# Second cross-attention in scaled half-precision parts, and its sum products behind a chunk's fourth score

## What is computed

```
x = x + tanh(g_xattn[0]) * L0_xattn(ln(x), ctx, mask)    # one head of 512, masked
x = x + tanh(g_ffn[0])   * L0_ffn(ln(x), w_up, w_down)   # Hadamard, 8 bit, ternary weights
x = x + tanh(g_xattn[1]) * L1_xattn(ln(x), ctx)          # 16 heads of channels
x = x + tanh(g_ffn[1])   * L1_ffn(ln(x), w1, w2, w3)     # silu(a) * b, NF4 weights
```

```
q = qkv.reshape(bs * 16, ch, length)
k = v = y.reshape(bs * 16, ch, -1)
scale = 1.0 / math.sqrt(math.sqrt(ch))
weight = softmax(einsum('bct,bcs->bts', q * scale, k * scale))
a = einsum('bts,bcs->bct', weight, v)
```

## Time and profile before

| | us |
|---|---|
| three runs | 1840.54, 1842.40, 1844.35 |
| median | 1842.4 |
| the profiled execution, its own time | 1841.3 |
| its span, first to last instruction | 1839.5 |
| PE busy in the span | 1658.9 (90%) |
| DVE, POOL, ACT busy | 1147.0, 843.0, 760.9 |
| mean granted clock of PE | 0.959 |

### The profile page before, as it was taken

How to read it: one execution, slowest core, us unless ns; L and a number is a source line. 1 busy time by engine, 2 the same in 40 slices (tenths; PEclk the granted TensorE clock), 3 DMA queues, 4 the chain that set the end, 5 groups by cost and what they waited for, 6 DMA issues and landing times. The chain is left out here.

```text
span 1839.5 us, 22129 instructions
## 1 busy us (share of the span) xinstructions
PE 1658.9 (90%) x7540; PEld 800.2 (44%) x7568; DVE 1147.0 (62%) x1529; ACT 760.9 (41%) x1241; POOL 843.0 (46%) x340
## 2 busy tenths in 40 slices
PE   5999999898777876899999999899999997799898
PEld 2454444444433333444444444444444432344443
DVE  3669989884455557676766676667676630444543
ACT  1321211211543431566666666566666665111110
POOL 0022234544221125577778888677777877000000
PEclk9999999899899995999999999999999999799999
DMA  8232223322111115444333334444433310400000
GB/s 320 80 120 77 83 93 96 103 100 79 39 30 35 34 41 137 113 114 112 77 96 89 98 97 113 114 113 113 113 88 90 77 46 1 95 23 0 23 23 23
DMA packets 134316, 152.57 MB, mean 83 GB/s; under 512 B 59694, under 2 KB 101826, under 8 KB 134214
## 3 DMA queue, kind: packets, MB, share of 16 engines
q1 hardware_dynamic: 129222, 140.76, 29.3%
q10 hardware_dynamic: 4992, 10.49, 1.7%
HBM read 73.42 MB, written 10.76 MB: 46 GB/s over the span
## 5 line engine op out<-in xcount | busy, mean ns | idle before, releaser
L1352 DVE TENSOR_REDUCE c_piece_max<-c_unit 128x1 f32<-128x804 f32 x512 | 485.0, 984 | 241.0 <-PE c_unit L1490 238.4
L1448 ACT ACTIVATE c_prob<-c_scores 128x512 f32<-128x512 f32 (+1 forms) x832 | 473.3, 596 | 267.3 <-PE c_scores L1507 250.5
L1287 POOL TENSOR_TENSOR c_prob_sum<-c_prob_sum,c_prob 128x2048 f32<-128x2048 f32 x96 | 439.4, 4577 | 12.0 <-ACT c_prob L1448 6.0
L1507 PE MATMUL c_scores<-c_queries,c_keys 98*128 98x512 f32 (+1 forms) x832 | 354.8, 443 | 32.7 <-ACT c_prob L1448 17.4
L1490 PE MATMUL c_unit<-c_khigh,c_qdiag 128*128 128x402 f32 x1024 | 303.2, 381 | 20.1 <-DMA c_qdiag<-c_qhigh 10.1
L1490 PEld LDWEIGHTS c_unit<-c_khigh,c_qdiag 128*128 128x128 f32 x1024 | 186.6, 198 | 150.1 <-DVE c_piece_max L1352 90.1
L1507 PEld LDWEIGHTS c_scores<-c_queries,c_keys 98*128 98x128 f32 (+1 forms) x832 | 152.4, 186 | 202.0 <-ACT c_prob L1448 141.3
L1516 PE MATMUL c_out<-c_prob,c_VT 128*32 128x512 f32 (+1 forms) x1664 | 220.8, 610 | 0.0
L641 PE MATMUL a_S<-a_ctxT,a_xnT 128*128 128x401 f32 x512 | 190.7, 517 | 7.2 <-ACT a_prob L598 3.9
L671 PE MATMUL a_o<-a_ctx,a_probT 128*128 128x512 f32 (+1 forms) x416 | 181.2, 592 | 0.0
L1287 POOL TENSOR_TENSOR c_prob_sum<-c_prob 128x2048 f32<-128x2048 f32 x16 | 73.5, 4592 | 121.1 <-ACT c_prob L1448 121.1
(11 more groups left out here) (196 smaller groups left out, 1975.0 us busy)
## 6 DMA issues: line engine op xcount, KB each, us to landing
c_keys<-c_khigh SPq DMA_DIRECT2D x128, 200.2 KB, 3.0
c_k<-in_keys SPq DMA_DIRECT2D x16, 801.0 KB, 6.3
c_keys<-c_k SPq DMA_DIRECT2D x64, 200.2 KB, 3.0
a_ctx<-in_ctx SPq DMA_DIRECT2D x12, 1024.0 KB, 6.8
c_VT<-in_values SPq DMA_DIRECT2D x16, 768.0 KB
a_ctxT<-in_ctxT SPq DMA_DIRECT2D x12, 802.0 KB, 4.7
c_queries<-c_qhigh SPq DMA_DIRECT2D x128, 64.0 KB, 2.6
a_weights<-in_L_ffn_weight SPq DMA_DIRECT2D x3, 1408.0 KB, 14.7
```

The source lines that it names most:

```text
L1287: nc.gpsimd.tensor_tensor(psum4[:], a[:], prob[(j * MC + c) % RING][:], ALU.add).then_inc(sums_taken, 2 if i == 1 else 1)
L1352: nc.vector.tensor_reduce(piece_max[j % 2][:, k // 2, k % 2:k % 2 + 1], U[bank(unit)][:, :, 0:PIECE], axis=AX.XY, op=ALU.max).then_inc(uni ...
L1448: nc.scalar.activation(prob[(j * MC + c) % RING][0:w, h, :], STp[h % 2][0:w, :], ACT.Exp, scale=SCALE).then_inc(exp_done, 1)
L1507: nc.tensor.matmul(STp[h % 2][0:w, :], K[p][:, h, c * P:c * P + w].bitcast(F32R), Q[p][:, h, :].bitcast(F32R), start=True, stop=True).then ...
```

## The change

1. In cross_attention_1 the tiles khigh, krest, qhigh, qrest, the query diagonal (QZ), K, Q and nrow are float16 in place of 32-bit types. krest no longer lies in the keys' own buffer. There is one row for the maxima in place of two (ones become 2^9, the row is divided by it), and no splitting of the maxima on ACT and POOL; `c_nmax` goes to PE.
2. So that the keys fit float16, they are multiplied by a scale of the whole context, 2^13 over its largest absolute value. ACT does so as it makes khigh; the exp gets its scale from a [128, 1] tile in place of a constant.
3. The scale is made in cross_attention_0: `context_top(b)` on DVE, for each batch, a transfer to memory and back over the partitions, and `context_scales()`, four small DVE operations. `load_transposed(b)` on SP waits for `context_top(b - 1)`.
4. `rest_of_k` goes from POOL to DVE: one scalar_tensor_tensor, in a slot's unit stream behind pair 6 of the group g+2. It is made in slots 0 to 13, and for groups 0 and 1 before them.
5. The sum products of a chunk in SUMMED go from behind its value products (after the second score) to behind the fourth score. The last chunk's stay.

The core of the diff:

```diff
-        krest = [k[:].bitcast(F32R) for k in kt]
-        khigh = [sb(f"c_khigh{j}", [P, MK], F32R) for j in range(2)]
+        krest = [sb(f"c_krest{j}", [P, MK], F16) for j in range(2)]
+        khigh = [sb(f"c_khigh{j}", [P, MK], F16) for j in range(2)]
...
+            def context_top(b):
+                for n in range(4):
+                    dve.wait_ge(ctxT_loaded[n], 16 * (b + 1))
+                nc.vector.tensor_reduce(ctx_tops[:, b:b + 1], CT[:], axis=AX.XY, op=ALU.max, apply_absolute_value=True).then_inc(ctx_topped, 1)
+                if b == B - 1:
+                    dve.wait_ge(ctx_topped, B)
+                    nc.vector.tensor_reduce(ctx_tops[:, B:B + 1], ctx_tops[:, 0:B], axis=AX.X, op=ALU.max).then_inc(ctx_topped, 1)
...
                 if k > 1:
                     add_out(k - 2)
+                if k % ST == 2:
+                    context_top(k // ST)
...
             add_out(K - 2)
+            context_scales()
...
-            def rest_of_k(n, j):
-                pool.wait_ge(khigh_ready, n + 1)
-                nc.gpsimd.tensor_tensor(krest[j], kt[j][:], khigh[j][:], ALU.subtract).then_inc(rests_ready, 1)
...
+            def rest_of_k(n, j):
+                dve.wait_ge(khigh_ready, n + 1)
+                wait(dve, stacked, (n - 1) * STACKS)
+                nc.vector.scalar_tensor_tensor(krest[j][:], kt[j][:], key_scale, khigh[j][:], ALU.mult, ALU.subtract).then_inc(krest_ready, 1)
...
+                    if main and more and unit[2:] == (j + 2, 6):
+                        rest_of_k(g + 2, j % 2)
...
-                nc.scalar.copy(khigh[j][:], kt[j][:]).then_inc(khigh_ready, 1)
+                nc.scalar.activation(khigh[j][:], kt[j][:], ACT.Copy, scale=key_scale).then_inc(khigh_ready, 1)
...
-                    nc.scalar.activation(prob[(j * MC + c) % RING][0:w, h, :], STp[h % 2][0:w, :], ACT.Exp, scale=SCALE).then_inc(exp_done, 1)
+                    nc.scalar.activation(prob[(j * MC + c) % RING][0:w, h, :], STp[h % 2][0:w, :], ACT.Exp, scale=score_scale[0:w]).then_inc(exp_done, 1)
...
-                        if h == 1:
-                            for b in outs.get(c, [c - 1]):
-                                out_and_den(g, j, b)
+                        for b in outs.get(c, [c - 1]):
+                            if h == 1:
+                                out_alone(g, j, b)
+                            elif h == 3:
+                                den_alone(g, j, b)
```

More of the change, by code:

```diff
@@ L1259, in rest_of_q @@
                 wait(pool, stacked, n * STACKS)
[L1260 to L1269 removed]
+                nc.gpsimd.tensor_tensor(qrest[:], xn[:], qhigh[j][:], ALU.subtract).then_inc(qrest_ready, 1)
             def add_gain(g):
@@ L1291, in _ @@
             rest_of_q(0, 0)
-            rest_of_k(0, 0)
             steps.link(pool.memset(QZ[1][:], 0.0))
@@ L1295, in _ @@
             rest_of_q(1, 1)
-            rest_of_k(1, 1)
             steps.link(pool.memset(ones32[:], 1.0))
             for j in range(2):
-                steps.link(pool.memset(K[j][KM:KA, :, :], 1.0))
-            rest_of_maxima(0)
+                steps.link(pool.memset(K[j][KM:KA, :, :], ONES))
             normalize(2)
@@ L1320, in slot @@
                     rest_of_q(g + 2, j % 2)
-                    rest_of_k(g + 2, j % 2)
             every_slot(pool, slot)
@@ L1361, in keep_rows @@
                 dve.wait_ge(unit_full, FULL0 + rows_place(n) + 1)
-                nc.vector.tensor_copy(nrow[:], U[bank(unit)][0:2 * H, 0, :]).then_inc(unit_read, 1)
+                nc.vector.tensor_scalar(nrow[:], U[bank(unit)][0:H, 0, :], 1.0 / ONES, None, ALU.mult).then_inc(unit_read, 1)
                 dve.wait_ge(unit_read, UNITS0 + rows_place(n) + 1)
@@ L1374, in _ @@
             statistics(1)
+            rest_of_k(0, 0)
             def slot(g, j, main, nxt, more, later):
@@ L1395, in slot @@
                         moments_done(g + 3)
+                    if main and more and unit[2:] == (j + 2, 6):
+                        rest_of_k(g + 2, j % 2)
                 if not main:
+                    rest_of_k(1, 1)
                     statistics(2)
@@ L1424, in split_queries @@
                 nc.scalar.copy(qhigh[j][:], xn[:]).then_inc(qhigh_ready, 1)
-            def high_of_maxima(n):
-                act.wait_ge(nmax_ready, n + 1)
-                wait(act, unit_full, FULL0 + rows_place(n - 1) + 1 if not isinstance(n, int) or n > 0 else 0)
-                nc.scalar.copy(nparts[:].bitcast(F32R)[:, :, :, 0].rearrange("p t h -> p h t"), nmax[:]).then_inc(nhigh_ready, 1)
             def take_out(g):
@@ L1465, in slot @@
                         split_keys(g + 2, j % 2)
-                    if c == (8 if not isinstance(g, int) or g > 0 else 10) and nxt:
-                        high_of_maxima(g + 1)
                 if nxt:
@@ L1489, in pair @@
                     at = STARTS[2 * half + e]
-                    last = nc.tensor.matmul(U[bank(unit)][:, e, 0:PIECE], QZ[o][:, h, t * P:(t + 1) * P].bitcast(F32R), khigh[o][:, at:at + PIECE], start=True, stop=True)
+                    last = nc.tensor.matmul(U[bank(unit)][:, e, 0:PIECE], QZ[o][:, h, t * P:(t + 1) * P], khigh[o][:, at:at + PIECE], start=True, stop=True)
                 last.then_inc(unit_full, 1)
@@ L1494, in rows @@
                 n = unit[1]
-                pe.wait_ge(nparts_ready, n + 1)
+                pe.wait_ge(nmax_ready, n + 1)
                 pe.wait_ge(unit_read, rows_place(n) + 1)
                 for t in range(TB):
-                    last = nc.tensor.transpose(U[bank(unit)][0:2 * H, 0, t * P:(t + 1) * P], nparts[:, t, :, :].rearrange("p h a -> p (h a)"), ident[:])
+                    last = nc.tensor.transpose(U[bank(unit)][0:H, 0, t * P:(t + 1) * P], nmax[:, t, :], ident[:])
                 last.then_inc(unit_full, 1)
@@ L1506, in score @@
                 pe.wait_ge(exp_done, g * EXPS + H * c + h + 1)
-                nc.tensor.matmul(STp[h % 2][0:w, :], K[p][:, h, c * P:c * P + w].bitcast(F32R), Q[p][:, h, :].bitcast(F32R), start=True, stop=True).then_inc(scores_ready, 1)
+                nc.tensor.matmul(STp[h % 2][0:w, :], K[p][:, h, c * P:c * P + w], Q[p][:, h, :], start=True, stop=True).then_inc(scores_ready, 1)
             def out(g, j, c):
@@ L1533, in den_of_sum, with out_alone, den_alone @@
                 last.then_inc(den_done, 1)
-            def out_and_den(g, j, c):
+            def out_alone(g, j, c):
                 last = out(g, j, c)
+                if c not in SUMMED:
+                    last.then_inc(pv_done, 1)
+            def den_alone(g, j, c):
                 if c in SUMMED:
-                    last = den(g, j, c)
-                last.then_inc(pv_done, 1)
+                    den(g, j, c).then_inc(pv_done, 1)
             def slot(g, j, main, nxt, more, later):
```

76 lines of the change are left out of this document (46 added, 30 removed).

## The result

The changed kernel takes 1863.14 us (median of 4 runs, 1861.71 to 1868.29) against 1841.89 us for the kernel before in the same comparison: a ratio of 1.0119, interval 1.0097 to 1.0141. It is slower by 21 us; 35 were forecast, and the range held it. The profiled execution took 1863.7 us, its span is 1861.9, 22.4 more than before.

A forecast was written before the change was run, and what follows sets the result against it. PE's order and exposed waits were taken to set the pace, POOL next. 1841.3 + 13.5 (cross_attention_0) - 5 (start) - 4 (slot 0) - 5 (slots 14, 15) + 37 (slots 1 to 13) = 1877.8, recorded as 1877; range 1808 to 1889.

The forecast's parts named there:

- The hold: Slots 1 to 13: DVE's rest-of-keys instruction waits for POOL's add-up, PE stands still 3.9 us; +3.65 us a slot.
- the rival that DVE slips through (B): cross_attention_1 slots: DVE isn't held by POOL's add-up, its 1.8 us hides in PE's two banks; 1812.2 us, chance 0.28.
- The clock: Slots 1 to 13: PE's stop brings its granted clock down, +1.4 us a slot, bounds 0 and 2.1.
- The steady slot without a hold: cross_attention_1, the edits together without any new wait: -2.2 us a slot.
- the pitch of 53.4: Sign that the forecast is right: a slot of cross_attention_1 lasts about 53.4 us; near 48 would mean not held.
- The sum products' move: Four chunks a slot: 0.42 of 0.97 us hidden behind the fourth score, -1.7 us a slot, bounds 0 and -3.
- Half precision with its slower exp: Faster score weight loads net of the exp's tile scale: -0.06 us a chunk, 9 plain chunks, -0.5 a slot.
- -0.15 a chunk: Scores and units in half precision: weight loads of 99 in place of 191 ns, once or twice a chunk, -0.15 us.
- The chain at tile 12: cross_attention_0: the reduction at k=10 passes whole by POOL and ACT to PE, +6.8 of +13.5 us.
- The start: cross_attention_1 before the scores: faster unit loads -2.3 us, maxima straight to PE -2.6; sum -5, bounds -3 and -6.
- Slots 0, 14 and 15: cross_attention_1: slot 0, with 49 units and its own long wait, -4 us; slots 14 and 15, without rest of keys, -5.
- rival A2: Slots 1 to 13: DVE held by POOL, but PE's clock stays up; 1859.6 us, chance 0.20.

The follow-up runs named there:

- e1: Changed kernel, with DVE's instruction for the rest of the keys reading one SBUF tile in place of two (krest then wrong): 1805.45 us, ratio 0.9815.
- e10: Changed kernel, with the real instruction for the rest of the keys in front of the third unit from the end of the slot's stream: 1806.00 us, ratio 0.9803.
- e6: The one-input variant of the changed kernel, with the sum products back behind the value products: 1822.51 us, ratio 0.9886.
- the run at the head: Changed kernel, with the rest of the keys in front of the first unit of the next slot: 1884.34 us, ratio 1.0224.

## Why the prediction was right, and where its numbers were off

**The hold.** Right as a mechanism, and the step on which the sign depended: the rival that DVE slips through (B) would have been 1812, and e1 and e10 show what it would have been with the hold alone gone, 1805 and 1806. The stop was put at 3.9 us a slot, it is 2.9. Three small errors add up: POOL's sum began 35.7 and ended 40.2 us into the slot, not 36.1 and 40.7; behind it DVE needed 1.7 us, not 1.8; and PE wanted its bank at 40.0, not at 39.6. Net 3.0 a slot in place of 3.65, 8 us in all.

**The clock.** I took 1.4 us in each of 13 slots, 18 in all, as one likeliest case and none as another. Neither is what happened: 8 of 13 stops came with the lower clock, which makes 16.4 us in all (the 55.4 of e1's comparison less 13 times 3.0), 2.05 on average, about 1.5 in a slot at 0.97 and 2.5 in one at 0.94. The granted clock of 748 to 1578 us is 0.96, where about 0.9 was given as a sign. With stops of 2.7 to 3.35 us this kernel is where a stop sometimes brings the clock down and sometimes not. The length alone does not decide: the stops of 2.70 and 2.69 us in slots 2 and 12 left the clock up, those of 2.68 in slots 3 and 13 did not. What does decide in a single slot stays open.

**The steady slot without a hold.** Forecast 2.2 us less than before, which is 48.1 from the usual 50.3; e1 and e10 measured 48.12 and 48.14. (The 50.58 that the prediction gives for a slot is the distance of two subtractions on POOL; from exp to exp slot 5 took 50.35. Its sum uses only changes, so nothing hangs on it but the pitch of 53.4 named as a sign; the mean was 52.5.) But the sum was right with two wrong terms whose errors happened to cancel, and that is luck. The sum products' move was put at -1.7 and is -0.67. Half precision with its slower exp was put at -0.5 and is -1.5 (50.3 before, 48.79 with the sums back), of which the exp's tile takes +0.90 (forecast +1.2 gross), so that the rest (halved loads, shorter waits and whatever else e6 shares with the change, not taken apart) gives -2.4. The prediction's own -0.15 a chunk would have been -2 in 13 chunks, but it was netted with the exp and applied to 9 of them only. For the move I could have read the room in the trace of before: PE's waits for exps before a score are 17.4 us in all its rows, and the 27 us expected of the move alone could not come out of them. In half precision these waits are 57.2 us, and 16.2 were filled.

**The loop's turn.** In the code slots 4 to 11 are a loop of two turns, and the second begins at slot 8. That slot took 55.93 us before, with the stop of the earlier trace rows and a granted clock of 0.94. Without the hold it takes 50.4 (e1): its longest stops of PE are 1.2 and 1.0 us, and the clock falls for a shorter time, 0.97 over the slot (0.55 from 1149 to 1151 us, 1.00 from 1153 on). That gave 5.6 us where 2.2 was forecast for each slot alike, and made the 13 slots gain 33.9 in place of 28.6 before the hold.

**cross_attention_0.** +16.1 for +13.5. The chain at tile 12 passed all of its 6.8 us (12.76 us of PE's waits for 5.83), and tile 15 has a wait of 4.29 us for +3.4. Of the other 4.9 us 3.1 lie ahead of PE's work at 342.55, where 3.3 were taken, and 1.8 behind it, where nothing was: after the stop in tile 15 the granted clock is 0.50 from 454 to 458 us, while in the kernel before it was 1.00 from 436 us to the function's end at 452. That this makes the 1.8 is an argument, not shown.

**The start.** -5.9 for -5: the wait before the transposes is 1.31 in place of 3.92 us, as forecast, and two units take 1.94 in place of 2.13 us, 0.19 where 0.14 was taken. But it was to come off the wait of 0.19 us for DVE, and that is still there; the four products take 1.75 in place of 1.94 us. **Slots 0, 14 and 15:** -9.4 for -9.

The total is 1863 for 1877: the hold 8 us less, the clock 2 less, the loop's turn 3, the other slots 2 and the start 1 better than forecast, against 2.6 more in the first function. It lies nearer to rival A2 (held, and the clock stays, 1859.6) than to the forecast, but not by A2's cause: the clock did fall in eight slots, and the hold was smaller than in both.

## What to carry to other kernels

Before an elementwise instruction with two inputs in SBUF goes from POOL to DVE, find where POOL stands at that moment; here the instruction's price was its own 1.9 us where POOL was idle, and about that plus the rest of POOL's instruction where it wasn't, and DVE then made all that it feeds late. Moving it by seven units of the stream, to a gap that the trace shows, turned 1.2% slower into 2% faster; but the gap must also be early enough for what hangs on the result, and that has to be followed through the queue of transfers. What reordering can hide in waits has as an upper bound the sum of these waits, which is a row of the trace; but it has to be the trace of the kernel in which the work will stand (17.4 us before, 57.2 once the scores were in half precision).

## What the runs showed of the hardware that I had not expected

- The hold goes both ways and catches the smallest instruction: a one-column operation on POOL took 1.77 us while DVE's ran, and 0.19 to 0.20 in e1, where DVE read one input.
- Of 13 stops of 2.68 to 3.35 us, 8 came with the lower clock; in the run at the head stops of 1.9 us did, too: after the one at 1026.8 the granted clock was 0.50 from 1030 to 1032.
- The granted clock of the whole trace is 0.959 before and 0.945 after; with the hold gone it is 0.956, and the lower clock is 16 us of the 55 that the hold costs.
